# Two-layer graph network with a tensor-product message stage: forming the last stage's node sums transposed

## The reference

```python
x0, x1 = _lin_irreps(x0, x1, W_up0, W_up1)          # 128 scalars and 128 vectors per node
h = edge_feats                                       # three small layers of width 64
tpw = h @ W_mlp4 / sqrt(64)                          # 512 weights per edge
w1, w2, w3, w4 = jnp.split(tpw, 4, axis=-1)
s0 = x0[sender]; s1 = x1[sender]
y0 = edge_attrs[:, 0:1]; y1 = edge_attrs[:, 1:4]
p1 = w1 * s0 * y0
p2 = (w2 * s0)[:, :, None] * y1[:, None, :]
p3 = w3[:, :, None] * s1 * y0[:, None, :]
p4 = w4 * jnp.einsum('eum,em->eu', s1, y1) / SQRT3
msg0 = segment_sum(concat([p1, p4]), receiver)       # 2*128 sums per node
msg1 = segment_sum(concat([p2, p3]), receiver)       # 3 * 2*128 sums per node
o0, o1 = _lin_irreps(msg0, msg1, W_out0, W_out1)
out = x + concat([o0, o1]) / 10
```

## Time and profile before

| | us |
|---|---|
| median of 3 runs | 5509.79 |
| the profiled execution | 5543.14 |
| its span | 5541.2 |
| last stage, first edge weights to last residual | 3242.5 to 5534.1 |

### The profile page before, as it was taken

One profiled execution on the slowest core, in us unless ns is written; L12 is line 12 of the kernel. 1 busy time (PEld: TensorE's weight loads), 2 busy tenths in 40 slices (PEclk: granted clock), 3 DMA queues, 4 the chain that ended last, 5 costly groups with the idle time before them and its releaser, 6 DMA issues.

```text
span 5541.2 us, 100657 instructions
## 1 busy us (share of the span) xinstructions
PE 4775.1 (86%) x15131; PEld 2045.2 (37%) x15183; DVE 2789.2 (50%) x6911; ACT 2209.7 (40%) x6164; POOL 2718.7 (49%) x3492
## 2 busy tenths in 40 slices
PE   6898557778899788887788889999999999999998
PEld 5443112233344223333334433333333334444443
DVE  7543112233444111113334457777777777777776
ACT  0442000011112222443222256666666666666665
POOL 0333666666665565445666634444444444333332
PEclk9999677789999889898989989999999999999999
DMA  2233566677776667667777744444444444444443
GB/s 82 95 108 106 174 183 205 205 223 229 232 245 215 193 205 212 197 193 222 238 247 249 264 122 126 122 125 127 123 128 120 130 123 126 125 123 122 128 122 106
DMA packets 433680, 916.88 MB, mean 165 GB/s; under 512 B 63093, under 2 KB 170869, under 8 KB 433510
## 3 DMA queue, kind: packets, MB, share of 16 engines
q0 software_dynamic: 195840, 641.89, 39.1%
q1 hardware_dynamic: 182918, 245.65, 13.1%
q10 hardware_dynamic: 54880, 28.91, 1.8%
HBM read 787.79 MB, written 128.41 MB: 165 GB/s over the span
## 4 chain that ended last, share of the span: by engine, by line
PE 35%; DVE 7%; issue 4%; DVEq 4%; another core or an unknown queue 3%; ACT 1%; DMA 0%; ACTq 0%; POOL 0%; SPq 0%; POOLq 0%
PE bank L1397 21%; PE bank L1387 6%; PE bank L1274 3%; DVE dense_w L1126 2%; PE bank L1333 1%; DVE hA L1117 1%; PE bank L1420 1%; DVE hA L1113 1%; PE bank L1421 1%; DVEq L281 1%; PE bank L1409 1%; DVE hB L1122 1%; DVEq L1120 1%; DVE hw L1154 1%
## 5 line engine op out<-in xcount | busy, mean ns | idle before, releaser
L547 POOL DMA_INDIRECT ring<-tab_d,idx x1568 | 1540.6, 983 | 852.1 <-issue 551.0
L1274 PE MATMUL bank<-ring,ohp 128*128 x3904 | 1131.5, 442 | 469.1 <-issue 222.8
L796 ACT ACTIVATE dense_w<-hA,hC 128x128 f32<-128x128 f32 x2640 | 819.3, 389 | 738.4 <-DVE hA L1113 628.2
L513 POOL DMA_INDIRECT ring<-up_d,idx x880 | 858.9, 976 | 498.5 <-POOL idx L509 347.6
L1397 PE MATMUL bank<-dense_w,yb 128*128 128x512 f32 x1760 | 934.5, 613 | 1.3 <-DVE dense_w L1130 1.1
L1397 PE MATMUL bank<-dense_w,oh 128*128 128x512 f32 x1760 | 898.7, 592 | 0.0
L1274 PEld LDWEIGHTS bank<-ring,ohp 128*128 x3904 | 415.0, 108 | 1158.0 <-issue 900.7
L1021 DVE TENSOR_TENSOR ohp<-iota_w,dst_f 128x512 f32 x392 | 267.3, 692 | 732.4 <-issue 259.8
L509 POOL COPY idx<-src_i 128x2 int32 x440 | 80.4, 183 | 885.1 <-DVE dense_w L1130 837.7
L1387 PE MATMUL bank<-w,hC 64*128 64x512 f32 x1760 | 498.3, 643 | 10.4 <-DMA hC<-hid_d 10.4
L1397 PEld LDWEIGHTS bank<-dense_w,oh 128*128 128x128 f32 x1760 | 334.4, 190 | 421.0 <-issue 421.0
(11 more groups left out here) (182 smaller groups left out, 5117.7 us busy)
## 6 DMA issues: line engine op xcount, KB each, us to landing
hC<-hid_d SPq DMA_DIRECT2D x440, 64.0 KB
tab_d<-tout SPq DMA_DIRECT2D x98, 256.0 KB, 2.8
tw<-tab_d SPq DMA_DIRECT2D x98, 256.0 KB
hlw<-hl_d SPq DMA_DIRECT2D x98, 256.0 KB
ring<-tab_d,idx POOLq DMA_INDIRECT x1568
hid_d<-hC ACTq DMA_DIRECT2D x98, 256.0 KB
hl_d<-agg SPq DMA_DIRECT2D x74, 256.0 KB, 3.0
ring<-up_d,idx POOLq DMA_INDIRECT x880
```

Of the source, the lines that this page charges most:

```text
L513: g_.indirect_dma_start(ring_v[:, b, k, :], None, table, bass.IndirectOffsetOnAxis(idx_t[:, b, k:k + 1], 0)).then_inc(S["got"][b], 16)
L547: g_.indirect_dma_start(ring_h[:, b, k, :], None, table, bass.IndirectOffsetOnAxis(idx_b[:, b, k:k + 1], 0)).then_inc(S["got"][b], 16)
L796: ac.mul(msg[:, b, k, 1, P + m * P:2 * P + m * P], t2[:, b, k, :], yg[:, b, 4 * k + 1 + m:4 * k + 2 + m])
L1274: ins = pe.matmul(bank[0][:, :], ohp_b[:, bass.ds(at, 1), k, :].rearrange("p b n -> p (b n)"), ring_b[:, bass.ds(slot, 1), k, h, :].rearra ...
```

## The change

In the last stage the roles of the operands are exchanged. The messages are stationary and the one-hots move, so a 128x128 piece of a sum comes out with the features on partitions and the nodes on columns, which is the form that the output product needs. The four pieces of bank 0 are four matmuls of 128 columns on the same moving `oh0`; the p4 piece is one of 128 columns on `oh`; the three p2 pieces have one common stationary `t2`, and move the one-hot times the three y1, which ScalarE now makes from `oh` instead of making the three products from `t2`. These three are one matmul of 384 columns. The total of streamed columns is the same.

There are two sets of accumulators, banks 0 and 1 and banks 6 and 7, used by alternate windows (`over_sets`). The first matmul of a window clears by its `start` flag. The copies to `mA` and `mB`, the clearing matmuls and the transposes are gone; `mT` is copied from the accumulators after the second pair of the next window, and the output product is written over the set's first bank. ScalarE now waits for the one-hot and no longer for `t2`. VectorE's and ScalarE's programs have plain loops over the first two pairs and the rest, and the range of the next window is read (`next_range`) after the copy to `mT`, no longer before the window's first pair.

```diff
-        def over_windows(eng, window):
-            window(0)
-            window(1)
-            with eng.Fori(2, NW - 1) as w:
-                window(w)
-            window(NW - 1)
+        def over_sets(eng, window):
+            window(0, 0)
+            window(1, 1)
+            with eng.Fori(1, NW // 2) as j:
+                window(j * 2, 0)
+                window(j * 2 + 1, 1)
+            window(NW - 1, 0)
...
-        m_bank = [bank[6], bank[7]]
+        sums = [(bank[0], bank[1]), (bank[6], bank[7])]
...
@@ ScalarE, weigh
-                    ac.wait_ge(M["t2"], n)
+                    ac.wait_ge(M["onehot"], n)
                     ac.wait_ge(M["seg_done"], n)
                     for k in range(2):
+                        ac.mul(oh0[:, b, k, :], oh[:, b, k, :], yg[:, b, 4 * k:4 * k + 1])
                         for m in range(3):
-                            ac.mul(msg[:, b, k, 1, P + m * P:2 * P + m * P], t2[:, b, k, :],
-                                   yg[:, b, 4 * k + 1 + m:4 * k + 2 + m])
-                    for k in range(2):
-                        ins = ac.mul(oh0[:, b, k, :], oh[:, b, k, :], yg[:, b, 4 * k:4 * k + 1])
+                            ins = ac.mul(msg[:, b, k, 1, P + m * P:2 * P + m * P], oh[:, b, k, :],
+                                         yg[:, b, 4 * k + 1 + m:4 * k + 2 + m])
...
@@ ScalarE and VectorE alike, a window (VectorE's has the rest below)
+            def copy_mT(w, p, behind=0):
+                ac.wait_ge(M["seg_done"], ac.snap(c) + (1 - behind))
+                after(ac, M["o_done"], w)
+                ac.copy(mT[:, 0:4, :], sums[p][0][:, :].rearrange("p (c n) -> p c n", c=4)).then_inc(M["mT_a"], 1)
+            def window(w, p):
+                lo, hi = ac.snap(lo_r), ac.snap(hi_r)
+                with ac.Fori(lo, lo + 2) as g:
+                    weigh(g)
+                if not isinstance(w, int) or w > 0:
+                    copy_mT(w - 1, 1 - p, 2)
+                if not isinstance(w, int) or w < NW - 1:
+                    next_range(w + 1)
+                with ac.Fori(lo + 2, hi) as g:
+                    weigh(g)
...
@@ VectorE, end of a window
                 ve.drain()
                 ve.tensor_scalar(iota_w[:, :], iota_w[:, :], float(P), None, ALU.add)
+                if not isinstance(w, int) or w > 0:
+                    finish(w - 1, 1 - p)
                 ve.drain()
...
@@ TensorE
-            def sum_pair(n, b, last):
+            def sum_pair(n, b, p, first):
                 pe.wait_ge(M["u_used"], n + NU)
-                pe.wait_ge(M["p2"], n + 1)
+                pe.wait_ge(M["scaled"], n + 1)
                 for k in range(2):
-                    for h in range(2):
-                        ins = pe.matmul(bank[h][:, :], (oh0, oh)[h][:, b, k, :], msg[:, b, k, h, :], start=False,
-                                        stop=(last and k == 1), skip_group_check=True)
+                    for i in range(4):
+                        pe.matmul(sums[p][0][:, i * P:(i + 1) * P], msg[:, b, k, 0, i * P:(i + 1) * P], oh0[:, b, k, :],
+                                  start=(first and k == 0 and i == 0), stop=False, skip_group_check=True)
+                    pe.matmul(sums[p][1][:, 0:P], msg[:, b, k, 1, 0:P], oh[:, b, k, :], start=(first and k == 0),
+                              stop=False, skip_group_check=True)
+                    ins = pe.matmul(sums[p][1][:, P:], t2[:, b, k, :], msg[:, b, k, 1, P:], start=False,
+                                    stop=False, skip_group_check=True)
                 ins.then_inc(M["seg_done"], 1)
-            def turn_m(w):
-                pe.wait_ge(M["mA"], w + 1)
-                pe.wait_ge(M["mB"], w + 1)
...
-                for i in range(8):
-                    sr = (mA if i < 4 else mB)[:, (i % 4) * P:(i % 4 + 1) * P]
-                    ins = pe.transpose(m_bank[i // 4][:, (i % 4) * P:(i % 4 + 1) * P], sr, ident[:, :])
-                ins.then_inc(M["turned"], 1)
...
             def window(w, p):
                 lo, hi = window_range(pe, w)
-                after(pe, M["mA"], w)
-                after(pe, M["mB"], w)
-                touch(bank[0][:, :], D, True)
-                touch(bank[1][:, :], D, True)
-                if not isinstance(w, int) or w > 0:
-                    turn_m(w - 1)
-                step(True)
...
+                if not isinstance(w, int) or w > 1:
+                    pe.wait_ge(M["out_ready"], w - 1)
+                step(p, first=True)
+                step(p)
+                if not isinstance(w, int) or w > 0:
+                    out_product(w - 1, 1 - p)
```

More of the change, by code:

```diff
@@ L32 @@
 LAG = 1
-MINV = 4
+MINV = 5
 NU = 4
@@ L184, in build @@
         q0 = hB[:, 1, :].rearrange("p (b k n) -> p b k n", b=2, k=2)
-        mA, mB, mT = agg, hw, AT
+        mT = AT
         def s(name):
@@ L775, in _ @@
             ac.wait_ge(hid_out, 16 * (NG // 4))
-            ac.nop().then_inc(M["p2"], 1)
+            ac.nop().then_inc(M["scaled"], 1)
             lo_r, hi_r = ac.alloc_register("act_tp_lo"), ac.alloc_register("act_tp_hi")
@@ L807, in first_pair @@
                 ac.reg_mov(hi_r, hi)
[L808 to L814, removed]
-                    weigh(g)
[L817 to L830, removed]
+            def copy_mT(w, p, behind=0):
[5 more added lines that the diff above has]
+                with ac.Fori(lo, lo + 2) as g:
+                    weigh(g)
                 if not isinstance(w, int) or w > 0:
-                    copy_mT(w - 1)
-                rest(w)
+                    copy_mT(w - 1, 1 - p, 2)
                 if not isinstance(w, int) or w < NW - 1:
-                    first_pair(w + 1)
-                keep_a(w)
-            first_pair(0)
-            over_windows(ac, window)
-            copy_mT(NW - 1)
+                    next_range(w + 1)
+                with ac.Fori(lo + 2, hi) as g:
+                    weigh(g)
+            next_range(0)
+            over_sets(ac, window)
+            copy_mT(NW - 1, 0)
         @block.vector
@@ L1132, in messages, with next_range @@
                 pick(ve, ve.snap(n % NU), 0, NU, pair)
-            def first_pair(w):
+            def next_range(w):
                 lo, hi = window_range(ve, w)
@@ L1137, in first_pair, with copy_mT, finish, window @@
                 ve.reg_mov(hi_r, hi)
-                messages(lo)
-            def second_pair(w):
-                messages(ve.snap(lo_r) + 1)
-            def rest(w):
-                with ve.Fori(ve.snap(lo_r) + 2, ve.snap(hi_r)) as g:
+            def copy_mT(w, p, behind=0):
+                ve.wait_ge(M["seg_done"], ve.snap(c) + (1 - behind))
+                after(ve, M["o_done"], w)
+                ve.tensor_copy(mT[:, 4:8, :], sums[p][1][:, :].rearrange("p (c n) -> p c n", c=4)).then_inc(M["mT_b"], 1)
+            def finish(w, p):
+                ve.wait_ge(M["x1_in"], (w + 1) * 16)
+                ve.wait_ge(M["o_done"], w + 1)
+                after(ve, M["stored"], w, 16)
+                ve.tensor_tensor(x1[:, 0:P], xw[:, 0:P], sums[p][0][:, 0:P], ALU.add)
+                ve.tensor_tensor(x1[:, P:].rearrange("p (v m) -> p v m", m=3), xw[:, P:].rearrange("p (v m) -> p v m", m=3),
+                                 sums[p][0][:, P:].rearrange("p (m v) -> p v m", m=3), ALU.add).then_inc(M["out_ready"], 1)
+            def window(w, p):
+                lo, hi = ve.snap(lo_r), ve.snap(hi_r)
+                with ve.Fori(lo, lo + 2) as g:
+                    messages(g)
+                if not isinstance(w, int) or w > 0:
+                    copy_mT(w - 1, 1 - p, 2)
+                if not isinstance(w, int) or w < NW - 1:
+                    next_range(w + 1)
+                with ve.Fori(lo + 2, hi) as g:
                     messages(g)
@@ L1147, in rest @@
                 ve.tensor_scalar(iota_w[:, :], iota_w[:, :], float(P), None, ALU.add)
+                if not isinstance(w, int) or w > 0:
+                    finish(w - 1, 1 - p)
                 ve.drain()
[L1150 to L1180 removed]
+            next_range(0)
             ve.drain()
[L1183 to L1186 removed]
+            over_sets(ve, window)
+            copy_mT(NW - 1, 0)
+            finish(NW - 1, 0)
         @block.tensor
@@ L1422, in out_product, with step @@
                 ins.then_inc(M["o_done"], 1)
-            def step(ahead, last=False):
+            def step(p, ahead=True, first=False):
                 n = pe.snap(c)
                 def one(b):
-                    sum_pair(n, b, last)
+                    sum_pair(n, b, p, first)
                     if ahead:
```

74 lines of the change are left out of this document (18 added, 56 removed).

## The result

| | median us | runs |
|---|---|---|
| before, on the same chip | 5509.32 (5499.64 to 5510.06) | 4 |
| after | 5606.40 (5596.39 to 5614.03) | 4 |

The ratio is 1.0174, 95% interval 1.0157 to 1.0192: slower by 97 us, where 90 us less was forecast, and outside the range. The profiled execution after took 5600.48 us, its span 5598.7.

A forecast was written before the change was run, and what follows sets the result against it. TensorE was taken to bound the last stage; -133 (borders), -1.9 (program's end), +35 (pairs) and +10 (border waits) gave -90 us, from a median of 5509.79 to 5420 us, range 5398 to 5480.

The forecast's parts named there:

- A pair on TensorE: Last stage, each pair's matmuls: 4.69 us becomes 4.77, +35 us over 440 pairs.
- a border's own 2.77 us: Window borders on TensorE: idling for copies, clearing and transposes all go, 48 x 2.77, -133 us.
- the output product: Once per window on TensorE: eight matmuls, 1.78 us, which also hide VectorE's copy and range reading.
- the slower rival: Weight loads not hidden on TensorE: short matmul instructions cost 0.19 us, not 0.111; +695 us, 6120 us; chance 0.07.
- ScalarE's copy and its changed wait: ScalarE, last stage: one copy less per window, starts on the one-hot, one product earlier; cost 0, no gain.
- The part on ScalarE and VectorE: What replaces the border: VectorE's drain and loop issue cost TensorE +10 us; ScalarE cost 0.
- Its own shortest round is 4412.31 - 4407.88 = 4.43 us, TensorE's is 4.77: 0.34 us free per pair: VectorE's round within a window, last stage: claimed shorter than TensorE's, leaving 0.34 us of slack per pair.
- VectorE paces the short windows: Rival for windows of five or six pairs: VectorE stalls TensorE 1.2 us per border, +58 us, 5480 us; chance 0.10.
- TensorE waits about 0.2 us per border: TensorE's wait for VectorE's last product at each border: 48 x 0.2, +10 us.
- The upper bound (0.7): TensorE's wait per border were VectorE's whole 3.27 us way across to remain: 0.7 us.
- The clock: TensorE's granted clock in the last stage: claimed to stay at 1.00.

The follow-up runs named there:

- less_dve: one_both with VectorE's product t2 left out: 5448.52 us, ratio 0.9833 to the kernel before.
- hidden_range: one_both with VectorE reading the next window's range inside the first two pairs' messages, ahead of a drain: 5385.11 us, ratio 0.9911 to the kernel before.
- one_both: The changed kernel with one window instead of two in VectorE's and ScalarE's loop bodies: 5458.82 us, ratio 1.0034 to the kernel before.
- one_pad: one_both with 256 small copies behind a never-taken branch in VectorE's loop body: 5911.41 us, ratio 1.0869 to the kernel before.
- before_two: The kernel before with two windows in VectorE's and ScalarE's loop bodies, nothing else changed: 5482.24 us, ratio 1.0075 to the kernel before.
- one_dve: The changed kernel with one window in VectorE's loop body alone, ScalarE keeping two: 5451.41 us, ratio 1.0016 to the kernel before.
- lean: one_both with the range read at the window's end and VectorE's mT copy moved to ScalarE: 5562.39 us, ratio 1.0041 to the kernel before.

## Why the prediction was wrong

The stage's length takes the sum apart. One step of the ladder is one difference of two traces:

| | stage us | step |
|---|---|---|
| predicted, and TensorE alone (less_dve 2205.7) | 2200 | |
| hidden_range | 2245.7 | +46: TensorE's waits at borders |
| one_both | 2305.1 | +59: the range's reading, with no slack on VectorE |
| after | 2394.7 | +90: VectorE's program is fetched |

**Right.** A pair on TensorE is 4.78 us (4.77 forecast), a border's own 2.77 us are gone, the output product is still 1.78. Weight loads are hidden, so the slower rival fell: the 24 loads of a pair, 0.19 to 0.20 us each, fit into its 4.78 us, and less_dve's TensorE is busy 699.97 of 700 us. The rule of the Trainium skill (TensorE: Matmul & The Clock Gate, "The mechanism") by which that rival was told, that a load overlaps a matmul only where their row groups differ, does not hold for these full-height tiles. ScalarE's copy and its changed wait were not tested by themselves, but less_dve, which has both, is within 6 us of the forecast.

**The step that failed first** is one that was never priced: `over_sets`. The part on ScalarE and VectorE spoke of plain loops, drains and loads, and took the form of the outer loop as nothing. It is worth 90 us (one_both), by branches out of a body that no longer stays resident: 53 us in which TensorE waits longer, and 36 by the clock that falls with the waiting. The forecast's 90 us of gain and this loss are of one size, so it alone would have given no change; the other two steps turned the sign.

**The second is "Its own shortest round is 4412.31 - 4407.88 = 4.43 us, TensorE's is 4.77: 0.34 us free per pair".** This took one of the four places of an unrolled loop, the quickest. The mean round was 4.64 in the kernel before and 4.8 in one_both, so 0.34 us of slack were 0.13 before and nothing in one_both. With no slack, the 2 us of copy and reading were not hidden by the output product: VectorE's program in one_both is 440 x 4.8 us, and 48 times 1.8 more at a border and 2.0 around the copy, 2294 us, and the stage is 2305.1. "VectorE paces the short windows" was the nearest rival and had 0.10; it was sized on the same 4.43 and gave 5480, still faster.

**The third is "TensorE waits about 0.2 us per border".** With 2.8 us assumed for VectorE's way across and 3.3 measured in hidden_range, it is 0.9 us in the mean: 44 us over the stage, not 10. The upper bound (0.7) rested on the same slack.

**The clock** was to stay at 1.00; it fell to 0.95 after and 0.90 in one_pad, and is 1.00 wherever TensorE doesn't wait long (one_both, less_dve, hidden_range). The forecast had no term for it.

So the idea of the change held and two of its side edits lost it. With one window per body and the reading of the range put under a drain, the same matmuls are 0.9% faster than the kernel before (interval 0.7 to 1.1%), where 1.6% was forecast.

## What to carry to other kernels

Before an engine's loop body is made longer, look at the instruction queues' packets and at how many instructions the body has. Here bodies of 204 and 259 instructions on VectorE ran without fetching, and those of 375, 463 and 516 fetched in every turn; some of their branches, one to three in a turn, then took about 3 us each, and a timeline shows that only as "issue". Measure an engine's own round as a mean over all copies of an unrolled body, and call it slack only if it stays positive after that. With two buffers between two engines the longest single round counted here, so work is best put where the engine waits anyway, not where the total looks smallest.

## What was not expected of the hardware

- A branch of VectorE behind which code is fetched took 1.9 to 4.3 us, with a median of 2.8 or 2.9 in each of three kernels (after, one_pad, before_two), though the transfers fill 0.1% of the DMA engines. 256 instructions that are never run made the kernel 8% slower than one_both.
- 111 packets more on ScalarE (one_dve against one_both) cost nothing, as ScalarE had a third of its time free.
- Behind each of the 22 waits of 4.0 to 6.8 us in after, the eight short instructions took 2.07 us instead of 1.15. Behind the 45 waits of 1.4 to 1.9 us in one_both they took 1.15 in 43 cases and up to 2.07 in two; the 1.90 behind 1.94 us in lean's rows above is such an exception.
- The same code of VectorE in another place of the program has issue gaps that differ by 0.1 to 0.2 us per round, even within one kernel (one_both), and the copies for its four buffers differ by up to 0.5 us.
